# High bf16 parts of eleven weight chunks written by casting DMAs on GpSimd's queue in place of ScalarE's copies

## The chip, the cores and the metric

One core of a Trainium2 chip. The time is that of the device in microseconds, the median of several executions. The engines are named as the profile names them: PE (TensorE, matrix products), DVE (VectorE), ACT (ScalarE), POOL (GpSimd, "Pool" in the text) and SP (SyncE, which here only issues DMAs).

## The reference

Two transformer layers on x of 8 x 256 x 256 (batch, tokens, width), in float32. Each adds to x an attention and a feed-forward part of the normalised x:

```python
xn = _layernorm(x)
x = x + _L0_attn_ref(xn, ...) + _L0_ffn_ref(xn, ...)
xn = _layernorm(x)
x = x + _L1_attn_ref(xn, ...) + _L1_ffn_ref(xn, ...)
```

Layer 0's attention is causal with 16 heads of 128 (w_q, w_k, w_v of 256x2048, w_o of 2048x256), its feed-forward part a gated GELU in fp8 with 1024 hidden units. Layer 1's attention has 16 heads of 16 (Wq, Wk, Wv, Wo of 256x256), its feed-forward part a gated SiLU with 1024 hidden units and two Hadamard transforms around it.

## The kernel before

Matrix products that must be near float32 run in bf16 with every operand split in two: a high part (the value rounded to bf16) and a low part (the value less its high part, rounded to bf16), and three products per pair (`PARTS`, line 613). So for each weight the kernel needs both parts in SBUF.

**Chunks of weights.** The weights come in 16 chunks (`chunks`, L174), most of 128 partitions x 2048 float32 (1 MB). `load_chunk` (L267), on SP's queue, writes a chunk to one of three stages in SBUF (`stage`). Three chunks are turned to fp8 by DVE. The other 13 are split in two halves each: `split_high` (L243) is a copy from the stage to the high part on ACT (L248), `split_low_dve` (L250) subtracts it from the stage on DVE for the first half (L258, stage and high part both in SBUF), `split_low_pool` (L261) does so on Pool for the second half (L265). ACT's copies count up one semaphore, `chunk_hi`; a low split waits for its own copy's count and for the stage, and its end frees the stage (`stage_free`), for which the next load into that stage and, by `weights_ready` (L723), PE's first use of the weight wait.

**Stages of the program.** Each engine has a setup and a program, and works them off in order. The setup (up to about 81 us) normalises x, transposes it and runs layer 0's feed-forward part in 32 tiles; the splits of qk 0 and v 0 are in its tiles 14 and 20, both halves low on DVE. Pool's setup (L349) is the reciprocal deviations (L352), the normalisation of x for pairs 1 to 3 (L360), and then four bias parts (`bias_parts`, L364 to L377) whose result DVE copies to `brow` as its last step of the setup (L552 to L556). SP's setup loads x, constants and the first chunks and stores x transposed and y.

The program (L963 on for PE, L1085 ACT, L1256 DVE, L1342 Pool, L1415 SP) goes slot by slot. In slot s head s of layer 0 is projected (q and k; v in even slots), the scores of head s-1 are taken, its probabilities are turned by DMA in the following slots, head s-3 is attended and head s-4 goes through w_o. 128 slots carry layer 0's 8 x 16 heads; layer 1 follows 16 slots behind. The queues of a slot s below 16, as far as the change touches them:

- PE: scores of head s-1 (waits for `qk0_lo`), q and k of head s, w_o of head s-4, v in even slots, attention of head s-3 (waits for SP's DMA transpose).
- ACT: high part of the output of head s-4 (L737), of p, the probabilities of head s-2 (L736, 128x384), exp of head s-1 (L995, waits for DVE's max), high parts of q and k (L737), the first copy of a chunk (L248), high part of v (L736, 128x512), the second copy of the chunk (L248).
- DVE: max of head s-1 (L1133), low part of the output (L742), low part of p (L741, 128x384, both operands in SBUF), reciprocal of the sums (L1156), low parts of q and k (L742), low part of v (L741, 128x512, one operand in PSUM), low split of a chunk (L258).
- Pool: normalisation of the probabilities of head s-1 (L1310, waits for the reciprocal), then the low split of the chunk's second half (L265), and from slot 15 on the folding of layer 1's weights (L1335).

`split_slot` (L182) gives each chunk's slot: wo0 0 in slot 0, qk 1 in 1, v 1 in 3, qk 2 in 4, qk 3 in 6, wo0 1 in 7, ug 0 in 8, ug 1 in 9, l1 in 11, dn in 13, wo1 in 15. `load_slot` (L185) gives the slot in which SP loads it. wo1 is half as large as the others.

Of the kernel before, what the change touches and what calls it, by code (L numbers as in the profile page):

```python
# [15 lines left out]
P = 128  # L16


def build(nc, t):
# [8 lines left out]
    KH = HID // P  # L28
# [8 lines left out]
    with ExitStack() as ctx:  # L37
# [3 lines left out]
        def sem(name):  # L41
            return ctx.enter_context(nc.semaphore(name))

        wqkv0 = sb("wqkv0", [P, 2, 3, KD, F0], BF16)
        wo0 = sb("wo0", [P, 2, H0, D], BF16)
# [118 lines left out]
        def upto(eng, semaphore, count):  # L164
            if count > 0:
# [10 lines left out]
        number = {c: n for n, c in enumerate(chunks)}  # L176
        dmas = {c: 2 if c[0] in ("qk", "g8") else 1 for c in chunks}
        loads_upto = {c: 16 * sum(dmas[chunks[z]] for z in range(n % STG, n + 1, STG)) for n, c in enumerate(chunks)}
        splits = chunks[3:]
        frees_upto = {c: sum(1 if chunks[z][0] in ("g8", "l8") else 2 for z in range(n % STG, n + 1, STG))  # L180
                      for n, c in enumerate(chunks)}
        split_slot = {("wo0", 0): 0, ("qk", 1): 1, ("v", 1): 3, ("qk", 2): 4, ("qk", 3): 6, ("wo0", 1): 7, ("ug", 0): 8,  # L182
# [1 line left out]
        split_tile = {("qk", 0): 14, ("v", 0): 20}  # L184
        load_slot = {("qk", 2): 1, ("qk", 3): 2, ("wo0", 1): 4, ("ug", 0): 5, ("ug", 1): 7, ("l1", 0): 8, ("dn", 0): 9,  # L185
                     ("wo1", 0): 10}
        stage_loaded = [sem(f"stage_loaded{i}") for i in range(STG)]
        stage_free = [sem(f"stage_free{i}") for i in range(STG)]
        x_loaded = [sem(f"x_loaded{i}") for i in range(RX)]
# [33 lines left out]
        def staged(eng, c):  # L223
            eng.wait_ge(stage_loaded[number[c] % STG], loads_upto[c])
# [16 lines left out]
            return tuple(v[:, j * n:(j + 1) * n] for v in (s, hi, lo))  # L241

        def split_high(act, c, j):  # L243
            staged(act, c)
            if c[0] == "dn":
                act.wait_ge(dn_sums, 2)
            s, hi, _ = half(c, j)
            nc.scalar.activation(hi, s, ACT.Copy, scale=SCALE1 if c[0] == "l1" and j == 0 else 1.0).then_inc(chunk_hi, 1)  # L248

        def split_low_dve(dve, c, j):  # L250
            dve.wait_ge(chunk_hi, 2 * splits.index(c) + j + 1)
            staged(dve, c)
            s, hi, lo = half(c, j)
            if c[0] == "l1" and j == 0:
                last = nc.vector.scalar_tensor_tensor(out=lo, in0=s, scalar=SCALE1, in1=hi, op0=ALU.mult,
                                                      op1=ALU.subtract)
            else:
                last = nc.vector.tensor_tensor(lo, s, hi, ALU.subtract)  # L258
            last.then_inc(stage_free[number[c] % STG], 1)

        def split_low_pool(pool, c, j):  # L261
            pool.wait_ge(chunk_hi, 2 * splits.index(c) + j + 1)
            staged(pool, c)
            s, hi, lo = half(c, j)
            nc.gpsimd.tensor_tensor(lo, s, hi, ALU.subtract).then_inc(stage_free[number[c] % STG], 1)  # L265

        def load_chunk(sp, c):  # L267
            name, k = c
            n = number[c]
            full, free = stage_loaded[n % STG], stage_free[n % STG]  # L270
            if n >= STG:
                sp.wait_ge(free, frees_upto[chunks[n - STG]])
            s = stage[:, n % STG, :]
            if name == "g8":
                d = s.rearrange("p (g k n) -> p g k n", g=2, k=KD)
                for z in range(2):
                    sp.dma_start(d[:, z], t["w_gating"][z].rearrange("(k p) n -> p k n", p=P)[:, :, k * 512:k * 512 + 512]
                                 ).then_inc(full, 16)
            elif name == "l8":
                sp.dma_start(s.rearrange("p (k n) -> p k n", k=KH), t["w_linear"].rearrange("(k p) n -> p k n", p=P)  # L280
                             ).then_inc(full, 16)
            elif name == "qk":
                d = chunk_view(c)[0]
                for w in range(2):
                    src = t[("w_q", "w_k")[w]].rearrange("(k p) n -> p k n", p=P)
                    sp.dma_start(d[:, w], src[:, :, k * 512:(k + 1) * 512]).then_inc(full, 16)
            else:
                if name == "v":
                    src = t["w_v"].rearrange("(k p) n -> p k n", p=P)[:, :, k * 1024:(k + 1) * 1024]
                elif name == "wo0":  # L290
                    src = t["w_o"].rearrange("(h p) n -> p h n", p=P)[:, k * 8:(k + 1) * 8, :]
                elif name == "l1":
                    src = t["w_qkv1"].rearrange("(k p) n -> p k n", p=P)
                elif name == "wo1":
                    src = t["wo1"]
                elif name == "ug":
                    src = t["w_ugT"][k * P:(k + 1) * P, :]
                else:
                    src = t["w_dnT"].rearrange("(k p) n -> p k n", p=P)
                sp.dma_start(chunk_view(c)[0], src).then_inc(full, 16)  # L300

        def sp_setup(sp):
            def load_x(p):
# [45 lines left out]
        def pool_setup(pool):  # L349
            def rstd_of(p):  # L350
                pool.wait_ge(var0, p + 1)
                nc.gpsimd.tensor_tensor(rstd[:, 4 * p:4 * p + 4], ve[:, 4 * p:4 * p + 4], mhalf[:, 0:4],  # L352
                                        ALU.pow).then_inc(rstd0, 1)

            def normalise(p):
                pool.wait_ge(rstd0, p + 1)
                upto(pool, xT_ps, p - 1)
                for i in range(4):
                    n = 4 * p + i
                    last = nc.gpsimd.tensor_scalar(xn[:, p % 2, i, :], xin[:, p, i, :], mv[:, n, 0:1], rstd[:, n:n + 1],  # L360
                                                   ALU.subtract, ALU.mult)
                last.then_inc(xn_ready, 1)

            def bias_parts(step):  # L364

                if step == 0:
                    pool.wait_ge(biases_loaded, 32)
                    nc.gpsimd.tensor_copy(bo_hi, bo).then_inc(bo_high, 1)
                elif step == 1:
                    pool.wait_ge(bo_high, 1)  # L370
                    nc.gpsimd.tensor_tensor(bo_rest, bo, bo_hi, ALU.subtract).then_inc(bo_left, 1)
                elif step == 2:
                    pool.wait_ge(bo_left, 1)
                    nc.gpsimd.tensor_copy(bo_mid, bo_rest).then_inc(bo_second, 1)
                else:
                    pool.wait_ge(bo_second, 1)
                    nc.gpsimd.tensor_tensor(bo_rest, bo_rest, bo_mid, ALU.subtract).then_inc(bo_left, 1)  # L377

            nc.gpsimd.memset(mhalf[:, :], -0.5).then_inc(half_ready, 1)
            nc.gpsimd.memset(ones[:, :], 1.0)  # L380
            nc.gpsimd.memset(brow[:, :, :], 0.0).then_inc(half_ready, 1)
            pool.wait_ge(half_ready, 2)
            rstd_of(0)
            rstd_of(1)
            normalise(1)
            for p in range(2, PAIRS):
                rstd_of(p)
                normalise(p)
            for step in range(4):
                bias_parts(step)  # L390

# [10 lines left out]
        def act_setup(act):  # L402
# [27 lines left out]
            for n in range(NT):  # L430
                p, k = divmod(n, KH)
                gate(n)
                if n:
                    gelu(n - 1)
                if k == 6 and p + 1 < PAIRS:
                    input_high(p + 1)
                if k == 1 and p >= 2:
                    output(p - 2)
                for c in splits:
                    if split_tile.get(c) == n:  # L440
                        split_high(act, c, 0)
                    if split_tile.get(c) == n - 2:
                        split_high(act, c, 1)
            gelu(NT - 1)

        def act_later_output(act, p):
# [4 lines left out]
        def dve_setup(dve):  # L451
# [73 lines left out]
            for n in range(NT):  # L525
                p, k = divmod(n, KH)
                linear_gate(n)
                if n >= 1:
                    product(n - 1)
                if n >= 2:  # L530
                    activation8(n - 2)
                if n in (0, 3):
                    statistics(2 + n // 3)
                if n in (1, 4):
                    variance0(2 + n // 3)
                if n == 1:
                    input_low(0)
                if n == 2:
                    float8(("l8", 0))
                if k == 5 and p + 1 < PAIRS:  # L540
                    input8(p + 1)
                if k == 7 and p + 1 < PAIRS:
                    input_low(p + 1)
                for c in splits:
                    if split_tile.get(c) == n:
                        split_low_dve(dve, c, 0)
                    if split_tile.get(c) == n - 2:
                        split_low_dve(dve, c, 1)
            product(NT - 1)
            for n in range(NT - 2, NT):  # L550
# [971 lines left out]
```

## Time and profile before

| | us |
|---|---|
| median of 3 runs | 908.67 |
| lowest, highest | 904.96, 912.39 |
| the profiled execution | 906.37 |
| its span, first to last instruction | 904.4 |
| busy in it: PE | 817.0 (90%) |
| DVE | 709.1 (78%) |
| ACT | 688.2 (76%) |
| POOL | 468.9 (52%) |

The granted clock of PE was 0.962 of full in the mean. The rows below name a line of the kernel, an engine, an operation and its operands; `arena` is the one SBUF buffer from which most tiles are carved, the stages among them. Times in the timeline are from the span's start.

### The profile page before, as it was taken

The page shows a single profiled execution, that of the slowest core. Times are in us where ns is not written, and L with a number is a line of the kernel's source. Part 1 is how long each engine was busy: PE and PEld are TensorE (multiplying, and loading weights), DVE is VectorE, ACT ScalarE, POOL GpSimd, SP SyncE. Part 2 cuts the span into 40 slices and gives each one's busy share as a digit, 9 for nine tenths or more (in the row PEclk, how much of TensorE's full clock was granted, in tenths as well). Part 3 has the DMA queues.
Part 4 walks back from the last instruction along what each step waited for, and adds up shares of the span by engine and source line. Part 5 has one row for each costly group of instructions (what it writes and reads, how often), then busy time and mean ns, then how long its engine had stood idle before and what let it go on. Part 6 is the DMA issues. An engine that isn't in the chain of part 4 may idle for free.

```text
span 904.4 us, 21144 instructions
## 1 busy us (share of the span) xinstructions
PE 817.0 (90%) x7072; PEld 604.2 (67%) x7072; DVE 709.1 (78%) x2027; ACT 688.2 (76%) x1985; POOL 468.9 (52%) x743
## 2 busy tenths in 40 slices
PE   3677888899999999999999999999999999998673
PEld 1344666677777777777777777777777777765341
DVE  6998797777878787878787878787877787875683
ACT  3587797666887888888888887888788878874673
POOL 4701455344456565555555655565555564665441
PEclk9899899999999999999999999999999999997885
DMA  9322776223455676466646755576467654663654
GB/s 309 114 82 85 182 182 167 44 41 97 74 95 83 126 110 111 83 123 115 109 76 125 112 106 83 115 119 110 78 121 121 106 83 96 125 114 74 121 111 92
DMA packets 286155, 99.92 MB, mean 110 GB/s; under 512 B 241504, under 2 KB 281696, under 8 KB 285664
## 3 DMA queue, kind: packets, MB, share of 16 engines
q1 hardware_dynamic: 286048, 98.58, 55.7%
q8 instruction: 57, 0.93, 0.5%
q14 instruction: 50, 0.41, 0.2%
HBM read 30.90 MB, written 8.91 MB: 44 GB/s over the span
## 4 chain that ended last, share of the span: by engine, by line
PE 68%; DVE 11%; ACT 4%; DMA 4%; issue 3%; SPq 1%; POOL 1%; POOLq 0%; ACTq 0%; DVEq 0%
PE ps L748 41%; PE ps L818 9%; PE ps L925 4%; PE ps L908 4%; PE ps L779 3%; DMA arena<-arena 3%; DVE arena L742 3%; PE ps L936 2%; DVE arena L1133 2%; PE ps L831 2%; PE ps L910 2%; DVE arena L741 1%; ACT arena L737 1%; ACT arena L995 1%; SPq L1407 1%
## 5 line engine op out<-in xcount | busy, mean ns | idle before, releaser
L742 DVE SCALAR_TENSOR_TENSOR arena<-ps,bqk,arena 128x256 bf16<-128x256 f32 x416 | 187.3, 479 | 45.8 <-ACT arena L737 44.7
L748 PE MATMUL ps<-arena,wqkv 128*128 128x256 bf16 x1728 | 217.1, 276 | 0.0
L737 ACT ACTIVATE arena<-ps,bqk 128x256 bf16<-128x256 f32 x416 | 178.2, 467 | 24.0 <-PE ps L748 14.8
L748 PEld LDWEIGHTS ps<-arena,wqkv 128*128 128x128 bf16 x1728 | 162.7, 99 | 42.1 <-issue 21.5
L1310 POOL TENSOR_SCALAR arena<-arena,rc 128x128 f32<-128x128 f32 (+1 forms) x256 | 106.3, 428 | 142.0 <-DVE rc L1156 142.0
L995 ACT ACTIVATE arena<-arena,nb 128x128 f32<-128x128 f32 (+1 forms) x256 | 114.5, 448 | 80.3 <-DVE nb L1133 79.9
L1301 POOL TENSOR_TENSOR arena<-arena 128x512 bf16<-128x512 f32 x107 | 124.9, 1167 | 71.3 <-ACT arena L736 71.3
L1317 POOL TENSOR_SCALAR arena<-arena,rc 128x256 f32<-128x256 f32 x256 | 119.8, 482 | 78.5 <-DVE rc L1160 78.4
L736 ACT ACTIVATE arena<-arena 128x384 bf16<-128x384 f32 (+1 forms) x256 | 136.9, 572 | 21.5 <-DMA arena<-arena 11.1
L995 ACT ACTIVATE arena<-ps,nb 128x256 f32<-128x256 f32 x256 | 118.5, 473 | 10.2 <-DVE nb L1140 8.0
L818 PE MATMUL ps<-wo,arena 128*128 128x256 bf16 x768 | 105.5, 274 | 13.2 <-DVE arena L742 12.5
L748 PE MATMUL ps<-wqkv,arena 128*128 128x512 bf16 (+1 forms) x480 | 105.7, 359 | 0.0
L748 PE MATMUL ps<-arena,wug 128*128 128x256 bf16 x768 | 97.9, 279 | 6.5 <-DVE arena L1199 6.5
L1133 DVE CUSTOM_DVE_ANT_0 arena<-ps,mask 128x128 f32<-128x128 f32 (+1 forms) x256 | 80.8, 353 | 28.9 <-PE ps L748 28.6
L741 DVE TENSOR_TENSOR arena<-arena 128x384 bf16<-128x384 f32 (+1 forms) x149 | 99.1, 670 | 1.8 <-ACT arena L736 1.8
L818 PEld LDWEIGHTS ps<-wo,arena 128*128 128x128 bf16 x768 | 71.8, 98 | 32.9 <-DVE arena L742 23.0
L748 PE MATMUL ps<-arena 128*128 128x128 bf16 (+1 forms) x768 | 85.0, 247 | 9.4 <-DVE arena L742 9.0
L1140 DVE TENSOR_REDUCE nb<-ps 128x2 f32<-128x512 f32 x128 | 86.4, 681 | 8.7 <-PE ps L779 8.6
L748 PEld LDWEIGHTS ps<-arena,wug 128*128 128x128 bf16 x768 | 75.9, 100 | 19.0 <-DVE arena L1199 7.9
L741 DVE TENSOR_TENSOR arena<-ps,arena 128x512 bf16<-128x512 f32 x80 | 54.7, 691 | 36.1 <-ACT arena L736 36.1
L748 PEld LDWEIGHTS ps<-wqkv,arena 128*128 128x128 bf16 x480 | 47.2, 98 | 33.3 <-issue 0.8
L748 PEld LDWEIGHTS ps<-arena 128*128 128x128 bf16 x768 | 56.0, 98 | 18.5 <-DVE arena L742 12.5
(108 smaller groups left out, 1220.8 us busy)
## 6 DMA issues: line engine op xcount, KB each, us to landing
arena<-scratch_qk SPq DMA_DIRECT2D x96, 64.0 KB, 2.6
arena<-arena SPq DMA_TRANSPOSE x256, 3.1
scratch_qk<-arena SPq DMA_DIRECT2D x32, 128.0 KB, 1.9
arena<-in_x SPq DMA_DIRECT2D x4, 512.0 KB, 8.7
arena<-in_w_gating SPq DMA_DIRECT2D x4, 512.0 KB, 7.2
arena<-in_w_q SPq DMA_DIRECT2D x4, 512.0 KB, 4.9
arena<-in_w_k SPq DMA_DIRECT2D x4, 512.0 KB, 5.8
arena<-in_w_v SPq DMA_DIRECT2D x2, 1024.0 KB, 6.7
```

Source lines behind the costliest of these rows:

```text
L736: return nc.scalar.activation(out, in_, ACT.Copy)
L737: return nc.scalar.activation(out, in_, ACT.Identity, bias=bias)
L741: return nc.vector.tensor_tensor(out, in_, hi, ALU.subtract)
L742: return nc.vector.scalar_tensor_tensor(out=out, in0=in_, scalar=bias, in1=hi, op0=ALU.add, op1=ALU.subtract)
L748: last = nc.tensor.matmul(out, lhsT, rhs, start=(n == 0), stop=(n == len(steps) - 1))
L818: last = nc.tensor.matmul(ps[:, BK_X, i * D:(i + 1) * D], oT0[:, a, n % 2, i * P:(i + 1) * P], wo0[:, c, h, :], start=False, stop=(h == H0 ...
L995: last = nc.scalar.activation(outs[i], ins[i], ACT.Exp, bias=bias[:, i:i + 1], scale=scale, accum_out=sums[:, i:i + 1])
L1133: last = nc.vector.tensor_tensor_reduce(out=sp0[:, n % 3, a:z], in0=ps[:, BK_S, a:z], in1=mask[:, a:z], scale=-SCALE0, scalar=3.0e38, op0= ...
L1140: nc.vector.tensor_reduce(nb1[:, n % 4, :], ps[:, score1_bank(n), :].rearrange("p (i k) -> p i k", i=TT), AX.X, ALU.max, negate=True).then ...
L1301: nc.gpsimd.tensor_tensor(pb1[:, n % RP1, 1, :, :, :].rearrange("p k i c -> p i k c"), p1[:, n % RP1, :, :].rearrange("p i (k c) -> p i k ...
L1310: last = nc.gpsimd.tensor_scalar(v, v, rc0[:, n % 4, i:i + 1], 1.0, ALU.mult, ALU.mult)
L1317: last = nc.gpsimd.tensor_scalar(v, v, rc1[:, n % 4, i:i + 1], 1.0, ALU.mult, ALU.mult)
```

## The change

For eleven of the 13 chunks (all but l1, whose first half is scaled, and dn, whose halves are first added and subtracted) the high part is no longer copied from the stage by ACT. Pool issues DMAs that read the weight in memory a second time and convert it to bf16 on the way, straight into the high part. All 15 of them (two for a qk chunk, one for each other) are issued in a row in Pool's setup, after the normalisation of the last pair and ahead of the bias parts. Each chunk has a semaphore of its own, for which the low splits wait. The loads to the stages by SP stay, as the low splits read them. ACT keeps the four copies of l1 and dn.

```diff
-        splits = chunks[3:]
+        splits = [("l1", 0), ("dn", 0)]
...
+        cast_loads = [("qk", 0), ("v", 0), ("wo0", 0), ("qk", 1), ("v", 1), ("qk", 2), ("qk", 3), ("wo0", 1), ("ug", 0),
+                      ("ug", 1), ("wo1", 0)]
+        high_loaded = {c: sem(f"high_loaded_{c[0]}_{c[1]}") for c in cast_loads}
...
         def split_high(act, c, j):
+            if c in high_loaded:
+                return
             staged(act, c)
...
+        def high_ready(eng, c, j):
+            if c in high_loaded:
+                eng.wait_ge(high_loaded[c], 16 * dmas[c])
+            else:
+                eng.wait_ge(chunk_hi, 2 * splits.index(c) + j + 1)
+
         def split_low_dve(dve, c, j):
-            dve.wait_ge(chunk_hi, 2 * splits.index(c) + j + 1)
+            high_ready(dve, c, j)
             staged(dve, c)
...
         def split_low_pool(pool, c, j):
-            pool.wait_ge(chunk_hi, 2 * splits.index(c) + j + 1)
+            high_ready(pool, c, j)
             staged(pool, c)
...
+        def load_high(pool, c):
+
+            hi = chunk_view(c)[1]
+            d = [hi[:, w] for w in range(2)] if c[0] == "qk" else [hi]
+            for dst, src in zip(d, chunk_source(c)):
+                pool.dma_start(dst, src).then_inc(high_loaded[c], 16)
...
             for p in range(2, PAIRS):
                 rstd_of(p)
                 normalise(p)
+            for c in cast_loads:
+                load_high(pool, c)
             for step in range(4):
                 bias_parts(step)
...
-                for c in splits:
-                    if split_tile.get(c) == n:
-                        split_high(act, c, 0)
-                    if split_tile.get(c) == n - 2:
-                        split_high(act, c, 1)
             gelu(NT - 1)
```

`chunk_source(c)` (new) returns the views of the weights in memory that `load_chunk` had inline; `load_chunk` now uses it and issues the same transfers as before.

## Rows read from the trace of the kernel before

**Rows 1.** Windows: stretch and length, busy us per engine (instructions), PE clock, DMA share, GB/s

```profile
36.00:81.00 45.00, 35.39 (x199) 19.63 (x200) 41.61 (x79) 32.78 (x55) 3.71 (x4) 0.92 0.30 94
81.00:131.00 50.00, 40.50 (x318) 29.58 (x316) 40.98 (x107) 41.33 (x94) 24.55 (x23) 0.93 0.65 155
...
200.00:300.00 100.00, 97.86 (x883) 76.44 (x882) 79.53 (x242) 78.17 (x236) 51.66 (x87) 1.00 0.47 86
```

(The engines are PE, PEld, DVE, ACT, POOL, in this order.)

**Rows 2.** One line's instructions, ACT's copies L248: ns least/median/most

```profile
L248 ACT ACTIVATE wqkv<-arena x14: 623/1048/1054, 47.8 to 141.4; 128x1024 bf16<-128x1024 f32 x13, 128x512 bf16<-128x512 f32 x1
```

**Rows 3.** The chain that ended last, 78 to 175 us: start, us, what

```profile
115.07 0.95 ACT wqkv L248
...
133.10 6.05 DMA scratch_y<-arena
...
162.42 0.63 ACT wo L248
```

**Rows 4.** Waits between 82 and 170 us: us in total, times, longest

```profile
ACT arena L995 <- DVE nb L1133: 10.8, 11, 3.1
```

**Rows 5.** Timeline of the setup: start, us, engine, line [idle before, releaser]

```profile
35.82 0.61 POOL L368 CAST arena<-arena 128x512 bf16<-128x512 f32 x1
...
48.85 1.22 DVE L258 TENSOR_TENSOR wqkv<-arena,wqkv 128x1024 bf16<-128x1024 f32 x1 [0.77 <-ACT wqkv L248]
...
56.35 1.46 SPq L314 DMA_DIRECT2D scratch_xT<-arena  x2
...
82.42 0.97 DVE L555 COPY brow<-arena 1x512 bf16<-1x512 bf16 x4
```

**Rows 6.** The page: DMA issues, KB each, median us from issue to landing

```profile
arena<-in_w_v SPq DMA_DIRECT2D x2, 1024.0 KB, 6.7
```

**Rows 7.** Groups: DVE 16-40 and 40-80 us, Pool 10-40 us, Pool whole span

```profile
L515 DVE CAST arena<-arena 128x512 fp8e4<-128x512 bf16 x8 | 5.4, 669 | 0.0
L515 DVE CAST arena<-arena 128x512 fp8e4<-128x512 bf16 x22 | 10.2, 463 | 0.0
L360 POOL TENSOR_SCALAR arena<-arena,mv,rstd 128x256 f32<-128x256 f32 x12 | 17.2, 1445 | 0.3
L1317 POOL TENSOR_SCALAR arena<-arena,rc 128x256 f32<-128x256 f32 x256 | 119.8, 482 | 78.5 <-DVE rc L1160 78.4
```

**Rows 8.** Timeline of slots 1 and 3, Pool's normalisation and the splits

```profile
88.77 0.82 POOL L1310 TENSOR_SCALAR arena<-arena,rc 128x128 f32<-128x128 f32 x2
90.07 1.23 DVE L258 TENSOR_TENSOR wqkv<-arena,wqkv 128x1024 bf16<-128x1024 f32 x1
91.07 2.21 POOL L265 TENSOR_TENSOR wqkv<-arena,wqkv 128x1024 bf16<-128x1024 f32 x1 [1.48 <-ACT wqkv L248]
...
98.98 0.83 POOL L1310 TENSOR_SCALAR arena<-arena,rc 128x128 f32<-128x128 f32 x2 [4.28 <-DVE rc L1156]
100.39 1.23 DVE L258 TENSOR_TENSOR wqkv<-arena,wqkv 128x1024 bf16<-128x1024 f32 x1
```

**Rows 9.** Timeline of slots 4 to 6, all engines

```profile
104.18 0.83 POOL L1310 TENSOR_SCALAR arena<-arena,rc 128x128 f32<-128x128 f32 x2 [0.59 <-DVE rc L1156]
107.46 1.22 DVE L258 TENSOR_TENSOR wqkv<-arena,wqkv 128x1024 bf16<-128x1024 f32 x1
107.84 2.81 POOL L265 TENSOR_TENSOR wqkv<-arena,wqkv 128x1024 bf16<-128x1024 f32 x1 [2.83 <-ACT wqkv L248]
109.54 1.53 DVE L741 TENSOR_TENSOR arena<-arena 128x384 bf16<-128x384 f32 x1
...
113.64 0.55 DVE L741 TENSOR_TENSOR arena<-arena 128x384 bf16<-128x384 f32 x1
114.45 1.46 PE L748 MATMUL ps<-wqkv,arena 128*128 128x512 bf16 x6
114.64 0.83 POOL L1310 TENSOR_SCALAR arena<-arena,rc 128x128 f32<-128x128 f32 x2 [2.57 <-DVE rc L1156]
...
117.18 1.22 DVE L258 TENSOR_TENSOR wqkv<-arena,wqkv 128x1024 bf16<-128x1024 f32 x1
```

More of the change, by code:

```diff
@@ L265, in split_low_pool, with chunk_source @@
             nc.gpsimd.tensor_tensor(lo, s, hi, ALU.subtract).then_inc(stage_free[number[c] % STG], 1)
+        def chunk_source(c):
+            name, k = c
+            if name == "g8":
+                return [t["w_gating"][z].rearrange("(k p) n -> p k n", p=P)[:, :, k * 512:k * 512 + 512] for z in range(2)]
+            if name == "l8":
+                return [t["w_linear"].rearrange("(k p) n -> p k n", p=P)]
+            if name == "qk":
+                return [t[w].rearrange("(k p) n -> p k n", p=P)[:, :, k * 512:(k + 1) * 512] for w in ("w_q", "w_k")]
+            if name == "v":
+                return [t["w_v"].rearrange("(k p) n -> p k n", p=P)[:, :, k * 1024:(k + 1) * 1024]]
+            if name == "wo0":
+                return [t["w_o"].rearrange("(h p) n -> p h n", p=P)[:, k * 8:(k + 1) * 8, :]]
+            if name == "l1":
+                return [t["w_qkv1"].rearrange("(k p) n -> p k n", p=P)]
+            if name == "wo1":
+                return [t["wo1"]]
+            if name == "ug":
+                return [t["w_ugT"][k * P:(k + 1) * P, :]]
+            return [t["w_dnT"].rearrange("(k p) n -> p k n", p=P)]
         def load_chunk(sp, c):
-            name, k = c
             n = number[c]
@@ L273, in load_chunk @@
             s = stage[:, n % STG, :]
-            if name == "g8":
+            if c[0] == "g8":
                 d = s.rearrange("p (g k n) -> p g k n", g=2, k=KD)
[L276 to L282, printed above, removed]
-                d = chunk_view(c)[0]
[L284 to L300, printed above, removed]
+                d = [d[:, z] for z in range(2)]
+            elif c[0] == "l8":
+                d = [s.rearrange("p (k n) -> p k n", k=KH)]
+            else:
+                d = chunk_view(c)[0]
+                d = [d[:, w] for w in range(2)] if c[0] == "qk" else [d]
+            for dst, src in zip(d, chunk_source(c)):
+                sp.dma_start(dst, src).then_inc(full, 16)
+        def load_high(pool, c):
+            hi = chunk_view(c)[1]
+            d = [hi[:, w] for w in range(2)] if c[0] == "qk" else [hi]
+            for dst, src in zip(d, chunk_source(c)):
+                pool.dma_start(dst, src).then_inc(high_loaded[c], 16)
         def sp_setup(sp):
@@ L543, in dve_setup @@
                     input_low(p + 1)
-                for c in splits:
-                    if split_tile.get(c) == n:
+                for c in split_tile:
+                    if split_tile[c] == n:
                         split_low_dve(dve, c, 0)
-                    if split_tile.get(c) == n - 2:
+                    if split_tile[c] == n - 2:
                         split_low_dve(dve, c, 1)
```

## The prediction

> **What bounds the kernel now.** I read the page's busy shares first, then the windows, then the chain and the waits, last the timeline of the stretch in which the copies run. Over the whole span PE is at 90% (the table of the time before), but that is an average of three stages. From about 165 us on PE hardly rests (97.9 of 100 us between 200 and 300) [rows 1], so what the first 165 us lose or win moves the end by as much. In the setup DVE is the bound: 41.6 of the 45 us from 36 to 81. In the first slots (81 to 131 us) nobody is: PE 40.5, DVE 41.0 and ACT 41.3 of 50 us [rows 1]. There a slot is a chain: scores on PE, max on DVE, exp and the high part of q, k on ACT, its low part on DVE, the next scores. Two slots take 9.7 us (DVE's split of slot 4 at 107.46, of slot 6 at 117.18) [rows 9].
>
> The copies of ScalarE look heavy: 22 go (20 of 128x1024, 2 of 128x512), 1.05 and 0.62 us each [rows 2], 22 us of ACT work. On the chain that ended last few of them stand: 0.95 us at 115 us (one like it 10 us later) and 0.63 us at 162 us [rows 3]. In the setup DVE waited 0.77 us for a copy at 48 us, and as long once more later [rows 5]. So their absence can win 1.5 + 1.9 + 0.7 = 4.1 us at most. Of ACT's own waits in these slots the largest is that of the exp for DVE's max, 10.8 us in 11 waits [rows 4]: ACT has slack, DVE's order decides.
>
> **Part 1, the setup.** (a) DVE's two waits go: -1.5 us [rows 5], if the high part of the first chunk has landed by 48.1 us (48.85 less 0.77). Pool issues it at about 35.8 us, where its bias parts now begin [rows 5]. A load of 1 MB takes 6.7 us to land [rows 6]; with two issues of 1.5 us (below) ahead, that is 35.8 + 3 + 6.7 = 45.5 us. In time.
>
> (b) Pool must issue 15 transfers (8 for qk, 2 v, 2 wo0, 2 ug, 1 wo1; 10.5 MB read) before its four bias parts. Those took 3.9 us (3.71 in the window from 36 us on, and 0.18 ahead of it) [rows 1, 5], and DVE wants them at 82.42 us [rows 5]. So there are 82.42 - 35.82 - 3.9 = 42.7 us, 2.8 us for each transfer, before anybody waits. The trace of before has no transfer issued by Pool. From below the nearest row is SP's issue, 1.46 us for two, 0.7 each; from above, Pool's longest split beside a busy DVE, 2.81 us [rows 5, 9]. I take 1.5 us, nearer to the first, because an issue moves no data through the engine: 22 us, hidden behind DVE's setup. At 2.81 us it is 42.2 us, just hidden.
>
> The Trainium skill (page "DMA: Bandwidth & Descriptors", section "Anatomy of one DMA — SWDGE (gpsimd) path") fits one such transfer at about 2.0 us plus its bytes over 436 GB/s, most of the 2 us being the wait for completion. By it the issues would be hidden too; no row here shows it.
>
> (c) Pool at work slows DVE. The cast of 128x512 to fp8 took 669 ns in the mean while Pool normalised (16 to 40 us) and 463 ns while it was idle (40 to 80 us) [rows 7]. In 22 us of issuing fall 12 such casts (22 in 40 us): 12 x 0.2 = 2.5 us if issuing disturbs like computing, 0 if not. I take 1.0.
>
> (d) Pool's half of the wo0 split no longer waits for ACT in slot 0. It runs as soon as the bias parts are done, beside the setup's DVE, and blocks one or two DVE instructions there: 0 to 2 us; by the 1.0 us by which a low part of p is drawn out beside Pool (below) I take 1.0.
>
> (e) The casting transfers share the 16 DMA engines with SP's loads and stores. These are busy 0.30 of the time from 36 to 81 us [rows 1], and SP's chunks are loaded many slots ahead: 0, up to 2 us if a store of xT lands late.
>
> Setup: -1.5 + 1.0 + 1.0 = +0.5 us, between -1.5 and +5.
>
> **Part 2, the slots.** What is new is the time at which Pool's low split runs. Before, it waited for ACT's second copy at the end of the slot. Now its high part has long landed, and it follows the normalisation (L1310) at once. That matters since DVE and Pool exclude each other when both read two SBUF operands. In slot 4 Pool's split ran from 107.84 to 110.65 us, and the low part of p, begun on DVE at 109.54, ended at 111.07 after 1.53 us; beside an idle Pool the same instruction takes 0.55 us [rows 9]. It did not slow down, it stood still until Pool was done.
>
> Slots without v. Slot 1: the norm ends at 88.77 + 0.82 = 89.59 us, and Pool's split (2.21 us there) would hold until 91.80. DVE's split began at 90.07 and would start at 91.80: +1.7 us, and DVE's next max is queued behind it, then ACT's exp [rows 8]. Slot 3: the norm ends at 99.81, Pool until 102.02, DVE's split wanted 100.39: +1.6 us [rows 8]. From each I take 0.2 off, as the low part of p no longer stands still behind Pool and ACT reaches its exp earlier: +1.5 and +1.4. Slot 7 the same: +1.5. Slot 9 too, but slot 10 waits for DMA anyway, below: I count +0.7.
>
> Slots with v: DVE's split comes later, behind the low part of v. Slot 4: the norm starts at 104.18, so Pool is done at 104.18 + 0.83 + 2.21 = 107.2, and DVE's split starts at 107.46: no loss. Slot 6: the norm ends at 115.47, Pool is done at 117.68, DVE's split wanted 117.18: +0.5, less 0.1 for the low part of p [rows 9]. Slot 8 the same. Together +0.8 us.
>
> Slots 9 and 10: SP's store of y (133.10 us, 6.05 us to land) stands on the chain [rows 3], and behind it a load of y, two loads of scales and the transpose that PE waits for. SP reaches that store after the low part of p of slot 8, whose standstill goes; so the half microsecond that DVE loses there is about returned, and a loss on DVE in slot 9 is partly covered by the DMAs. That is my reason for halving it.
>
> Slot 15: Pool's split of wo1 waited for ACT's 0.63 us, and DVE for the fold behind it [rows 3]. Pool can start at the end of its norm: -0.7 us.
>
> Copies on the chain at 115 and 125 us: each stands ahead of the high part of v. PE ended v at 114.45 + 1.46 = 115.91 us [rows 9], the copy at 116.02 [rows 3], so -0.1 each.
>
> The splits of l1 and dn (slots 11 and 13) stay. Slots: 1.5 + 1.4 + 1.5 + 0.7 + 0.8 - 0.7 - 0.2 = +5.0 us. Bounds: if Pool's start does not block DVE, the slots win 2.6 us (the 4.1 above less the setup's 1.5); if PE, idle longer in four slots, also runs longer at the lower of its two clocks (0.93 of full is granted here against 1.00 later [rows 1]), they lose 10.
>
> Sum: the profiled execution took 906.37 us; 906.4 + 0.5 + 5.0 = 911.9 us. The median of the three runs before is 908.67 us, against which that is +0.4%. I give 912.
>
> **The rivals.** *The copies held the slots.* For: ACT is 41.3 of 50 us busy, as busy as DVE. Against: its exp waits for DVE's max. If Pool's early start does not block DVE: 906.4 - 4.1 = 902.3 us.
>
> *Pool issues too slowly* (this one ends slower). The bias parts stand behind 15 issues, and DVE's last work of the setup behind them; it decides from 2.8 us per transfer. For: Pool's normalisation of 128x256 took 1445 ns beside a busy DVE, another scaling of 128x256 on Pool takes 482 ns later on, so an issue could be drawn out threefold too [rows 7]. Against: nothing in these rows ties an issue to DVE's operands. At 4 us each the bias parts end at 35.8 + 60 + 3.9 = 99.7 us, 17.3 us after DVE wants them: 912 + 17 = 929 us.
>
> The Trainium skill (page "SBUF — State Buffer", the box on "The DVE blocks DMA trap") has a rule of this kind against the change: GpSimd writes the descriptors of a transfer that it issues, and cannot while DVE runs certain copies and casts. The threefold stretch of Pool's own instructions agrees in kind; no transfer of before was issued that way.
>
> *The casting transfers are slow.* Chunks land in order, and the tightest is ug0, the ninth MB: its split is due in slot 8, at 117.2 + 9.7 = 126.9 us [rows 9], so 91 us from 35.8 on, 10 us per MB. Against: 6.7 us for a whole MB alone [rows 6]. At twice that, ug0 lands at 35.8 + 9 x 13.4 = 156.4: +29 us, 941 us.
>
> **How the numbers follow.** Chances: forecast 0.62 (own range 905 to 919), copies held the slots 0.17, Pool issues too slowly 0.15, slow transfers 0.06. The range, 902 to 928, takes in the second case and the milder half of the third. One per cent of the median is 9.1 us (899.6 to 917.8), about what a measurement of this kernel can tell from none. Faster than that needs more than the chain has to give: 0.05. Slower: the two slow cases and a tenth of the forecast, 0.27. Within 1%: 0.68.
>
> **What would show it.** L248 left with 4 activations. In slots 1, 3, 7: Pool's L265 right behind L1310, DVE's L258 drawn out to 2.5 us or more, and L741 (128x384) at 0.55 us in nearly all slots. DVE's first two splits without a wait. Pool's bias parts done before 78 us. Wrong: L258 stays at 1.22 us with Pool's split begun before it (then the time is near 902), DVE waits for Pool at L555 (near 929), or a split waits for a DMA.

## The result and the profile after

| | kernel before | changed kernel |
|---|---|---|
| median, us (4 runs each) | 906.85 | 919.49 |
| lowest, highest | 904.96, 912.39 | 913.52, 921.54 |
| ratio, 95% interval | | 1.0093 [1.0064, 1.0123] |
| the same kernel once more (`a1_again`, 10 runs) | 910.2 | 915.76 |
| ratio, 95% interval | | 1.0057 [1.0037, 1.0077] |
| span of the profiled execution | 904.4 | 919.7 |

By the ratios the change costs 0.6 to 0.9%: slower, as forecast (912, +0.4%), and by more than forecast. The recorded ratio is not the quotient of the two medians; for the first comparison that quotient is 1.014, outside the interval, and for `a1_again` 1.006. With four runs on each side the first comparison is the weaker of the two. Two of the ten runs of `e3_both` below (919.2 and 926.1 us) count as slow and are left out of its median and its ratio. The profiled execution lies 15.3 us above that of before, and its trace says where these were lost. The lines of the kernel have moved: L248 is L253 now, L258 L269, L265 L276, L411 (high part of x transposed) L434, L736 L754, L741 L759, L1133 L1151, L1310 L1328.

The page of the changed kernel: busy time, and the queues of the DMA engines. Queue q0 is new, it is Pool's.

```profile
PE 812.9 (88%) x7006; PEld 604.2 (66%) x7072; DVE 710.6 (77%) x2027; ACT 667.8 (73%) x1963; POOL 475.6 (52%) x758
...
q1 hardware_dynamic: 286048, 98.58, 55.4%
q0 software_dynamic: 5232, 5.51, 3.6%
```

ACT is 20.4 us less busy (688.2 before), 1963 instructions in place of 1985: the 22 copies are gone, as they should be. DVE is as busy as before. 5.51 MB were written by Pool's transfers, for twice as much read (all reads from HBM rose from 30.90 to 41.91 MB).

The windows show the stage that lost most (columns as in [rows 1]):

```profile
36.00:81.00 45.00, 28.09 (x149) 15.09 (x150) 35.18 (x62) 21.49 (x36) 17.48 (x20) 0.80 0.97 200
81.00:131.00 50.00, 39.26 (x286) 27.33 (x288) 38.54 (x101) 28.35 (x73) 13.30 (x16) 0.91 0.49 125
...
200.00:300.00 100.00, 96.63 (x867) 75.67 (x874) 80.43 (x245) 76.01 (x229) 51.01 (x84) 1.00 0.45 79
```

From 36 to 81 us DVE, the bound of the setup, falls from 41.6 to 35.2 us, and the DMA engines go from 0.30 busy to 0.97. The waits of the setup name the cause (waits between 36 and 93 us: us in total, times, longest):

```profile
ACT arena L439 <- PE ps L617: 14.4, 17, 4.1
...
DVE arena L526 <- ACT arena L444: 10.7, 7, 8.6
ACT arena L434 <- DMA scratch_xT<-arena: 10.3, 1, 10.3
```

One wait of 10.3 us: ACT, about to write the next x transposed into its buffer, waits for SP's store of the one before. DVE waits 8.6 us behind ACT in its turn. The timeline has the place, after it the same instruction of the kernel before:

```profile
63.43 0.62 ACT L444 ACTIVATE arena<-arena 128x512 bf16<-128x512 bf16 x1
74.40 1.02 ACT L434 ACTIVATE arena<-ps 128x1024 bf16<-128x1024 f32 x1 [10.35 <-DMA scratch_xT<-arena]
```

```profile
64.12 1.02 ACT L411 ACTIVATE arena<-ps 128x1024 bf16<-128x1024 f32 x1 [1.48 <-DVE arena L487]
```

Up to there both kernels are level: DVE begins the same tile's copy at 67.23 us and at 67.26 before. The setup's end, measured by DVE's split of wo0 in slot 0, moved from 85.58 to 94.21 us: 8.6 us lost by this one wait.

Slots 1 and 3, Pool's normalisation and the two low splits (the counterparts of [rows 8]):

```profile
97.30 0.83 POOL L1328 TENSOR_SCALAR arena<-arena,rc 128x128 f32<-128x128 f32 x2 [43.58 <-DVE rc L1174]
98.10 2.12 POOL L276 TENSOR_TENSOR wqkv<-arena,wqkv 128x1024 bf16<-128x1024 f32 x1
98.54 2.76 DVE L269 TENSOR_TENSOR wqkv<-arena,wqkv 128x1024 bf16<-128x1024 f32 x1
101.78 0.55 DVE L759 TENSOR_TENSOR arena<-arena 128x384 bf16<-128x384 f32 x1
...
108.50 2.13 POOL L276 TENSOR_TENSOR wqkv<-arena,wqkv 128x1024 bf16<-128x1024 f32 x1
108.96 2.75 DVE L269 TENSOR_TENSOR wqkv<-arena,wqkv 128x1024 bf16<-128x1024 f32 x1
```

This is what the forecast had said line for line: Pool's split right behind its normalisation, DVE's split begun during it and drawn out from 1.23 to 2.76 us, the low part of p back at 0.55 us. Both long splits stand on the chain that ended last (start, us, what), and DVE's next max comes straight behind them:

```profile
98.62 2.68 DVE wqkv L269
101.30 0.20 DVE arena L1151
...
109.04 2.66 DVE wqkv L269
```

From Pool's normalisation of slot 1 to that of slot 16 it was 79.9 us before (88.77 to 168.69) and is 85.8 us now (97.30 to 183.10): 5.9 us. With the 8.5 us by which slot 1 already began late and 0.9 after slot 16 that is the whole 15.3. These are single executions, and the figure for the slots is the less certain one: `b1_first` below, which has the old splits, took 83.6 us for the same slots in its profiled execution.

### The profile page after: what moved, and what is told of

It is laid out like the page before. It is cut to its first block, busy times and chain, and to the rows that moved or that the text cites. A ratio compares the mean times of both kernels' runs of the same rounds, so it can differ in the third digit from the quotient of the medians.

```text
span 919.7 us, 21071 instructions
## 1 busy us (share of the span) xinstructions
PE 812.9 (88%) x7006; PEld 604.2 (66%) x7072; DVE 710.6 (77%) x2027; ACT 667.8 (73%) x1963; POOL 475.6 (52%) x758
## 3 DMA queue, kind: packets, MB, share of 16 engines
q0 software_dynamic: 5232, 5.51, 3.6%
HBM read 41.91 MB, written 8.91 MB: 55 GB/s over the span
## 4 chain that ended last, share of the span: by engine, by line
PE 67%; DVE 12%; ACT 4%; issue 4%; DMA 3%; POOL 1%; SPq 1%; POOLq 0%; ACTq 0%; DVEq 0%
PE ps L766 40%; PE ps L836 9%; PE ps L943 4%; PE ps L926 3%; PE ps L797 3%; DMA arena<-arena 3%; DVE arena L760 3%; PE ps L954 2%; DVE arena L1151 2%; PE ps L849 2%; PE ps L928 2%; ACT arena L755 1%; ACT arena L1013 1%; DVE arena L759 1%; DVE wqkv L269 1%
## 5 line engine op out<-in xcount | busy, mean ns | idle before, releaser
L766 PE MATMUL ps<-arena,wqkv 128*128 128x256 bf16 x1728 | 214.6, 274 | 0.0
L1328 POOL TENSOR_SCALAR arena<-arena,rc 128x128 f32<-128x128 f32 (+1 forms) x256 | 105.5, 424 | 205.4 <-DVE rc L1174 205.4
L755 ACT ACTIVATE arena<-ps,bqk 128x256 bf16<-128x256 f32 x416 | 177.6, 465 | 24.9 <-PE ps L766 13.8
L754 ACT ACTIVATE arena<-arena 128x384 bf16<-128x384 f32 (+1 forms) x256 | 136.5, 571 | 22.2 <-DMA arena<-arena 12.7
L1151 DVE CUSTOM_DVE_ANT_0 arena<-ps,mask 128x128 f32<-128x128 f32 (+1 forms) x256 | 80.7, 352 | 28.3 <-PE ps L766 27.8
L766 PE MATMUL ps<-wqkv,arena 128*128 128x512 bf16 (+1 forms) x426 | 94.8, 359 | 2.8
L766 PE MATMUL ps<-arena 128*128 128x128 bf16 (+1 forms) x768 | 85.0, 247 | 10.9 <-DVE arena L760 10.7
L759 DVE TENSOR_TENSOR arena<-arena 128x384 bf16<-128x384 f32 (+1 forms) x149 | 92.0, 622 | 1.0 <-ACT arena L754 1.0
L759 DVE TENSOR_TENSOR arena<-ps,arena 128x512 bf16<-128x512 f32 x80 | 54.6, 690 | 36.5 <-ACT arena L754 36.5
```

Source lines behind the costliest of these rows:

```text
L754: return nc.scalar.activation(out, in_, ACT.Copy)
L755: return nc.scalar.activation(out, in_, ACT.Identity, bias=bias)
L759: return nc.vector.tensor_tensor(out, in_, hi, ALU.subtract)
L766: last = nc.tensor.matmul(out, lhsT, rhs, start=(n == 0), stop=(n == len(steps) - 1))
L1151: last = nc.vector.tensor_tensor_reduce(out=sp0[:, n % 3, a:z], in0=ps[:, BK_S, a:z], in1=mask[:, a:z], scale=-SCALE0, scalar=3.0e38, op0= ...
L1328: last = nc.gpsimd.tensor_scalar(v, v, rc0[:, n % 4, i:i + 1], 1.0, ALU.mult, ALU.mult)
```

## The experiments

All times are medians; the ratio is to the kernel before on the same chip. Two edits undo one loss each, `e1_turn` the blocking and `e4_first` the stall.

**e1_turn: Pool's split behind DVE's again.**

```diff
                 for c in splits_in[s]:
+                    if v_in(s) is None:
+                        pool.wait_ge(qk0_lo, s + 1)
+                    else:
+                        pool.wait_ge(v0_lo, v_in(s) + 1)
                     split_low_pool(pool, c, 1)
```

> The changed kernel with one edit: Pool's low split of a chunk also waits until DVE has done its low part of v (slots with v) or of q and k (others), so that DVE's split begins first, as before the change. Theory 'Pool first blocks DVE': DVE's splits in slots 1, 3, 6 to 9 fall from 2.75 and 1.46 us to 1.22 us, and of the 5.9 us that slots 1 to 15 lost some 5 come back; Pool's half of wo0 also leaves the setup and DVE's cast of 2.34 us beside it falls to 0.42. The stall of ACT at about 64 us stays. Time some 5 us (0.5%) below the changed kernel's 919.5, about 914. Rival 'the slots lost their time to something else (the lower clock of PE after the setup's stall, DMA traffic)': the splits get shorter but the slots still take 80 us or so from slot 1 to slot 15, and the time stays at 919.

Measured: 913.67 us, 1.0053 [1.0029, 1.0078]. That is the time expected, but against the 1.0057 of `a1_again` this edit alone won nothing that can be told; what the blocking costs shows between e4_first and e5_turn_first. Slot 1 in its trace:

```profile
98.09 1.21 DVE L269 TENSOR_TENSOR wqkv<-arena,wqkv 128x1024 bf16<-128x1024 f32 x1
98.25 3.03 POOL L276 TENSOR_TENSOR wqkv<-arena,wqkv 128x1024 bf16<-128x1024 f32 x1 [0.49 <-DVE arena L760]
99.77 1.93 DVE L759 TENSOR_TENSOR arena<-arena 128x384 bf16<-128x384 f32 x1
```

DVE's split is at 1.21 us, Pool's takes 3.03 as it now stands still first, and the low part of p is drawn out again, which costs little. Slots 1 to 15 take 78.5 us (96.94 to 175.39), 7.3 less than in the changed kernel. Who begins first decides who waits, and it matters only where the chain runs. The stall at L434 stays, 9.6 us.

**e2_late: six chunks' casts in the slots, not in the setup.**

```diff
-            for c in cast_loads:
+            for c in cast_loads[:5]:
                 load_high(pool, c)
...
                 fold(s)
+                for c, z in zip(cast_loads[5:], (1, 2, 4, 5, 6, 8)):
+                    if z == s:
+                        load_high(pool, c)
```

> The changed kernel with the casting transfers of the last six chunks (qk 2, qk 3, wo0 1, ug 0, ug 1, wo1) issued by Pool in slots 1, 2, 4, 5, 6 and 8 in place of its setup; 7 of the 15 transfers (5 of 10.5 MB) stay in the setup. Theory 'the store of x transposed stands behind the volume in flight': the casts are done by about 36 + 5/10.5 x 38 = 54 us, the two stores issued at 56.6 land in 3 to 7 us, ACT's wait of 10.4 us at L434 is gone and the setup ends 8 us sooner (about 84.5 us): 911 us. Rival 'the stores are slow beside any transfer of Pool's, or the stall has another cause': ACT still waits at L434 and the time stays at 919. The later casts land in 3 to 7 us each when alone; if they take over 12 us, a split waits for one.

Measured: 913.64 us, 1.0058 [1.0026, 1.0089]. The stall is gone (the stores landed in 6.2 us, the split of wo0 on DVE stood at 83.61 us), but the time fell less than expected, and against `a1_again` not at all: the casts now run beside the DMA transposes that the slots need. The transposes of layer 0 up to 165 us land in 4.2 us in the median and 12.8 at most (2.8 and 6.2 before), PE waits 9.2 us for them, and Pool itself 5.2 us for a cast of wo0 1. I had counted casts in the slots as free.

**e3_both: e1_turn and e2_late together.** Its diff is the two above.

> Both edits of e1_turn and e2_late. If the two losses are apart and are all: 919.5 - 5 - 8 = 906, and below that by what the absence of ScalarE's copies is worth, which I had put at 4.1 us at most: 902 to 906, against 906.9 before the change. Rival 'the copies cost nothing where they stood': 906 to 908. If it stays above 912 a third loss is open.

Measured: 911.11 us, ratio 1.0017 [0.9985, 1.0049]: a miss, as against 902 to 906. Waits between 82 and 185 us:

```profile
ACT arena L1013 <- DVE nb L1151: 23.0, 18, 4.1
PEld ps L926 <- DMA arena<-arena: 15.0, 7, 3.2
PE ps L926 <- DMA arena<-arena: 12.2, 7, 2.9
```

L926 is the attention of layer 0, waiting for the transposed probabilities: 12.2 us, where it was 0.9 before the change. Slots 1 to 15 took 84.8 us in place of the 78.5 of e1_turn. The third loss is of this edit's own making, and the DMA engines' time is as real a resource in the slots as in the setup.

**e4_first: the store of x transposed first on SP's queue.**

```diff
+            store_x(2)
             load_chunk(sp, ("qk", 1))
             store_y(0)
-            store_x(2)
```

> The changed kernel with one edit on SP's queue: the store of x transposed of pair 2 is issued ahead of the load of qk 1 and the store of y, at about 51 us in place of 56.6. All casts stay in flight until 74 us. Theory A 'the DMA engines share their time between SP's and Pool's rings': alone at the head of SP's ring the store lands in 5 to 9 us, by 60 us, ACT does not wait at L434, the setup ends 8 us sooner: about 911 us. Theory B 'a store lands only when the writes queued before it, Pool's too, are done': the store was issued behind all 15 casts and still lands at about 74 us: ACT waits as before, 919 us.

Measured: 910.58 us, ratio 1.0017 [0.9991, 1.0042]. With all casts in flight, the two stores landed in 7.6 us (issues at 51.9 us, median from issue to landing; the engines wholly busy in that stretch):

```profile
q0 software_dynamic: 648, 0.83, 118.3%
...
scratch_xT<-arena SPq DMA_DIRECT2D x2, 256.0 KB, 7.6
```

ACT's wait at L434 is 0.5 us and for DVE, the split of wo0 stands at 85.28 us. Theory B falls: a store does not wait for the casts queued before it. It takes its turn among them, and what made it late in the changed kernel was that plus the 1 MB of qk 1 and the 256 KB of y ahead of it in SP's own queue.

**e5_turn_first: both losses undone.** Its diff is that of e1_turn and that of e4_first.

> Both edits of e1_turn and e4_first, all casts in Pool's setup as in the changed kernel. By the traces of those two: the setup ends with the split of wo0 on DVE at about 84.5 us (85.28 in e4_first, less 1 us since Pool's half of wo0 is back in slot 0), slots 1 to 15 take 78.5 us as in e1_turn (79.9 before the change), the rest 735.8: 902 us against a median of 908.8 with 904.4 in the profiled span, that is 0.2 to 0.3% below the kernel before. Theory 'the copies of ScalarE are worth something once nothing else is lost': ratio to the kernel before below 1, 0.997 or so. Rival 'they are worth nothing': ratio 1.000 or above, slots 1 to 15 at 80 us.

Measured: 904.59 us, 0.9944 [0.9917, 0.9971]: faster than the kernel before. DVE's splits are at 1.21 to 1.30 us in the slots; the slots take 80.2 us, not 78.5. So the ratio came out as the theory had it and the slots as the rival had them; where the gain sits is taken up below.

**e6_turn_gap: the late casts issued once the store has landed.**

```diff
-            for c in cast_loads:
+            for c in cast_loads[:5]:
                 load_high(pool, c)
             for step in range(4):
                 bias_parts(step)
+            pool.wait_ge(xT_stored, 64)
+            for c in cast_loads[5:]:
+                load_high(pool, c)
```

(with e1_turn's edit; SP's order as before.)

> e1_turn with the casts of the last six chunks issued after the bias parts and once the store of x transposed of pair 2 has landed (Pool waits for it), SP's order unchanged. Theory 'volume in flight under that store': it lands at about 62 us, Pool issues the rest from 62 to 68, 5.5 MB read are done by 80 us, ahead of the first DMA transpose at 93 us. Setup as in e5_turn_first, slots 78.5 us: 902 us. Against e2_late and e3_both this shows whether it was the casts beside the transposes that cost the slots there (DMA waits of PE 11 to 15 us): here such waits should be back at 3 us or less. If the setup still ends late, ACT waits at L434 or at L449 (store of y).

Measured: 905.94 us, 0.9948 [0.9921, 0.9974]. Pool's second batch:

```profile
62.99 0.75 POOL L321 DMA_DIRECT2D wqkv<-in_w_q  x1 [17.64 <-DMA scratch_xT<-arena]
...
67.92 0.55 POOL L321 DMA_DIRECT2D wo<-in_wo  x1
```

PE's waits for transposes are back at 2.1 us in these slots; in the kernels that have no casts beside the transposes they lie between 0.6 and 5.7 us, against 9.2 and 12.2. So it was the casts beside the transposes that cost e2_late and e3_both their gain, and volume in flight under the store that cost the changed kernel its setup: the same eight transfers, issued 22 us later (the first at 62.99 us in place of 41.20), cost neither.

**b1_first: SP's order alone, on the kernel before.** The edit of e4_first.

> Control: the kernel before the change with e4_first's edit on SP's queue alone (store of x transposed of pair 2 ahead of the load of qk 1 and the store of y). In the kernel before ACT did not wait for that store, so the order should be worth nothing: ratio 1.000 within 0.2%. If it comes out at 0.997 or lower, the gain of e5_turn_first is SP's order and not the copies.

Measured: 907.24 us, 0.9985 [0.9958, 1.0011]: no difference that can be told, as expected. By itself it leaves e5_turn_first a gain of 0.4% over it with about as much uncertainty; e6_turn_gap, which keeps SP's order, stands at 0.9948 as well. The other edit of these kernels, Pool's split behind DVE's, was not run on the kernel before, where Pool's split already began after DVE's.

**a1_again: the changed kernel unaltered.**

> The changed kernel once more, unaltered, since four runs of it stand so far (919.5, ratio 1.0093) and the edits are read against it. e1_turn (0.5% above the kernel before), e4_first (0.2% above) and e5_turn_first (0.6% below) give 11 us... worked out: taking the stall as e1_turn less e5_turn_first, 1.09%, and the blocking as e4_first less e5_turn_first, 0.73%, the changed kernel should stand 0.994 + 1.1 + 0.7 = 1.2% above the kernel before if the two losses simply add, 920 us; if one hides part of the other, between 0.7 and 1.1%, 915 to 919 us.

Measured: 915.76 us, 1.0057 [1.0037, 1.0077]; in its trace ACT waits 7.6 us at L434, and DVE's splits of slots 1, 3, 7 and 9 take 2.75 us or more. The two losses do not add up: 1.09% (e1_turn less e5_turn_first) and 0.73% (e4_first less e5_turn_first) make 1.8%, and the changed kernel stands 1.1 to 1.5% above e5_turn_first. Each of these figures is uncertain by 0.3 to 0.4, so I don't read a mechanism into it; why undoing the blocking wins 0.7% once the stall is gone and nothing that can be told before stays open.

**e7_all: e5_turn_first and e6_turn_gap in one.**

> e5_turn_first and e6_turn_gap in one: Pool's split behind DVE's, the store of x transposed of pair 2 first on SP's queue, the last six chunks' casts only once it has landed. Both reach the same setup end, so if stall and blocking are all that was lost, this adds nothing to either: 0.994 to 0.996 of the kernel before, 904 to 906 us. In e5_turn_first ACT still waited 2.3 us at L449 for the store of y behind the casts; if such waits matter the ratio falls to 0.992.

Measured: 906.91 us, 0.9957 [0.9935, 0.9979]: nothing on top of either, as expected.

## Why the prediction was right, and where it was off

Right was the sign, the range (902 to 928 holds 919.5 and 915.8), and by the ratios (0.93 and 0.57%) that the change stays within 1%; the first median, 919.5, lies above the 917.8 at which I had put the end of that band, and just outside the 905 to 919 of the forecast case. The mechanism of part 2 carried it. By its steps:

- **The copies are worth little** (4.1 us at most). With both losses undone the casts win 0.43 to 0.56% (e5, e6, e7), 4 to 5 us, each give or take 2 to 2.5 us. The bound was of the right size. Where these microseconds arise is shown only in part. Slots 1 to 15 of those three kernels take 80.2, 80.5 and 84.2 us against 79.9, but up to slot 12 (table below) they and e1_turn are some 1.3 us shorter in the mean than the kernels with copies, with e6_turn_gap no shorter at all. Part is in the setup, where in e6_turn_gap DVE's path from its first split to that of wo0 is 35.7 us against 36.7.
- **(a) DVE's two waits go**: yes; the first part was there in time (DVE's first split starts at 46.25 us without a wait).
- **(b) 15 issues**, 1.5 us each, 22 us, hidden: they took 10.9 us (35.71 to 46.60), 0.6 to 0.97 us each. The hidden part held with much room; the rival "Pool issues too slowly" is out. The rule of the Trainium skill that I had weighed there (page "SBUF — State Buffer", "The DVE blocks DMA trap") has GpSimd unable to write a transfer's descriptors while DVE runs certain copies and casts. In this trace no such standstill is seen: the issues during which an fp8 cast of DVE began (at 37.40, 39.01 and 40.49 us) took 0.72, 0.77 and 0.73 us, no longer than their neighbours.
- **(c) and (d) Pool beside DVE in the setup**, +1.0 each. The price in (c) rested on a misreading. The mean of 669 ns over the eight casts between 16 and 40 us was not made by Pool's normalisation, beside which they took 0.41 to 0.52 us; two casts beside the additions of the bias parts made it (kernel before):

```profile
32.52 0.41 DVE L515 CAST arena<-arena 128x512 fp8e4<-128x512 bf16 x1
...
36.51 1.20 POOL L371 TENSOR_TENSOR arena<-arena 128x512 f32<-128x512 f32 x1
36.63 1.37 DVE L515 CAST arena<-arena 128x512 fp8e4<-128x512 bf16 x1
```

  So the bias parts cost DVE about 2 us already before the change; now they run 11 us later and cost it 1.1. The issues cost DVE little (two fp8 casts at 0.60 and 0.64 us, then 0.41 to 0.43). New is Pool's split of wo0 in the setup:

```profile
51.34 2.38 POOL L276 TENSOR_TENSOR wo<-arena,wo 128x1024 bf16<-128x1024 f32 x1
51.66 2.34 DVE L533 CAST arena<-arena 128x512 fp8e4<-128x512 bf16 x1
```

  a cast of 0.42 us stands for 1.9 us behind Pool's split. Together with the issues that is 2.3 us more than before, less 1 us for the cheaper bias parts and 1.5 us for (a): DVE's fourth split starts at 66.09 us, against 66.12.
- **(e) The shared DMA engines: "0, up to 2 us"**. This is the step that failed: 8.6 us. I read the mean busy share (0.30 over 45 us) and SP's loads, "many slots ahead", and not the one transfer whose end somebody waits for soon after. The trace of before has it, in the transfers issued between 56.3 and 58 us:

```profile
scratch_xT<-arena SPq DMA_DIRECT2D x2, 256.0 KB, 6.1
```

  The second of the two stores was issued at about 57 us and landed 6.3 us later, at about 63.4, and ACT writes its buffer anew at 64.12: the margin was less than a microsecond, however idle the engines were in the mean. With Pool's backlog around it the same stores took 16.2 us (issues between 54 and 58 us of the changed kernel):

```profile
q0 software_dynamic: 907, 0.81, 125.4%
...
arena<-in_w_q SPq DMA_DIRECT2D x1, 512.0 KB, 6.5
arena<-in_w_k SPq DMA_DIRECT2D x1, 512.0 KB, 10.9
scratch_xT<-arena SPq DMA_DIRECT2D x2, 256.0 KB, 16.2
scratch_y<-arena SPq DMA_DIRECT2D x1, 256.0 KB, 15.2
```

- **Slots without v, 1.4 to 1.5 us each; with v +0.4**: DVE's split took 2.76 us in slot 1, 2.75 in slots 3, 7 and 9, 1.21 in slot 4, 1.45 and 1.46 in slots 6 and 8. Forecast were +1.7, +1.6, +1.5, about +1.5, 0, +0.5, +0.5 before deductions; measured +1.5 four times, 0, +0.2, +0.2.
- **Sum of the slots +5.0 us**: 5.9 in the profiled execution, but between traces it varies. From Pool's normalisation of one slot to that of another (us, one profiled execution each; e2_late and e3_both, with casts in the slots, left out):

| | slots 1 to 12 | slots 12 to 16 |
|---|---|---|
| copies on ACT, not blocked: before, b1_first | 56.5, 56.4 | 23.4, 27.2 |
| casts, blocked: changed kernel, a1_again, e4_first | 60.5, 58.9, 60.5 | 25.3, 22.6, 23.2 |
| casts, not blocked: e1_turn, e5_turn_first, e6_turn_gap, e7_all | 53.9, 55.3, 56.4, 55.0 | 24.5, 24.9, 24.1, 29.2 |

  The splits whose order the change turns round lie in slots 1 to 9 (that of slot 15 apart), and up to slot 12 the blocked kernels stand apart from all others: blocking costs 3.5 us on the mean against the kernels with copies (forecast for this part: 5.7) and 4.8 against the casts alone. The figures from slot 12 on do not follow the groups. Per slot the drawn-out split is in part won back by the next slot: slot 1 takes 5.9 us in place of 5.1, slot 2 then 4.5 in place of 5.1. By medians the blocking is worth 0.73% (e4_first less e5_turn_first), 6.6 us, give or take 3.
- **The chances**: 0.68 within 1%, 0.27 slower. The forecast case itself was right in kind; what came on top of it was a case I had folded into a term of zero.

Against a forecast of +5.5 us the medians of the first comparison give +12.6 (its ratio 8.4) and those of the second +5.6. The agreement of the second is in part luck: its trace holds the stall that I had put at nothing (7.6 us of ACT's wait, the split of wo0 at 93.39 us), and its slots lost 1.5 us in place of 5. The sum was near; one of its terms was not.

## What to carry to other kernels

A copy taken off an engine pays at most what its waits and its pieces on the chain show, here 4 us of 22. An operand that arrives early also lets its reader start early: look at which engine the freed instruction now meets, and whose chain stands behind it; a wait that looks like waste can be what keeps the order right. Bulk transfers put into a quiet stretch are to be checked against each transfer whose end somebody waits for soon, by its own landing time and margin there, and not against the mean share of the DMA engines. Here it helped to put that one first on its own queue (e4_first), or to issue half of the bulk once it had landed and early enough to be done before the next urgent ones (e6_turn_gap). A mean over instructions beside a busy engine says little about what slows them: look at the single ones.

## What the runs showed that I had not expected

- Pool issues a casting transfer of 512 KB or 1 MB in 0.6 to 1.0 us. Fifteen of them, 11 MB read and 5.5 MB written, kept the 16 DMA engines nearly always busy from 36 to 74 us; the first landed after 6.3 us, the last 28.1 us after its issue.
- Beside such a backlog SP's transfers take their turn: the pair of stores of 256 KB that took 7.6 us alone at the head of SP's queue took 16.2 us behind 1.25 MB of SP's own. They do not wait for the casts issued before them.
- Casts beside DMA transposes stretch these from 2.8 to 5.8 us in the median (e3_both, up to 165 us), and PE waited 12.2 us for them.
- PE's clock around the stall: granted 0.50 of full, its lower level of 1.2 GHz, in the 5 us in which PE stood idle behind ACT and in the 5 us after (0.78 from 81 to 86 us, then 1.00):

```profile
71.00:76.00 5.00, 0.03 (x1) 0.03 (x2) 0.00 (x0) 1.60 (x3) 0.00 (x0) 0.50 0.76 277
76.00:81.00 5.00, 3.76 (x9) 1.14 (x10) 4.42 (x9) 3.58 (x6) 0.00 (x0) 0.50 0.04 12
```

  Most of it was hidden behind DVE: the setup ended 8.6 us late after DVE had stood still for 8.6.
